# Scores of all nodes kept in SBUF and stored once, and clears and weight loads moved between stages, in a fused graph network

## What is computed

```python
x = _layernorm(x + _L0_gnn_ref(x, edge_index, ...))   # two GAT layers and a matmul with Wu
x = _layernorm(x + _L1_gnn_ref(x, W_fc, attn_l, attn_r, W_res, src, dst))
x = _layernorm(x + _L2_gnn_ref(x, edge_index, W, b))  # GCN
x = _layernorm(x + _L3_gnn_ref(x, W1, b1, W2, b2, edge_index))  # two GCNs

def _L1_gnn_ref(h, ...):
    hh = h.reshape(n, 12, 64)
    ft = einsum('nhd,ed->nhe', hh, W_fc)
    a1, a2 = (ft * attn_l).sum(-1), (ft * attn_r).sum(-1)   # scores of a node: 12 + 12
    e = leaky_relu(a1[src] + a2[dst]); softmax of e over the edges of a target
    return relu(einsum('nhd,ed->nhe', hh, W_res) + sum over edges of alpha * ft[src])
```

## Time and profile before

| | us |
|---|---|
| median of 3 runs | 3817.73 (3816.74 to 3828.18) |
| the profiled execution | 3819.96 |
| its span | 3818.0 |
| TensorE busy in the span | 3544.9 (93%) |
| VectorE | 2428.9 (64%) |
| ScalarE | 1380.7 (36%) |
| GpSimd | 1112.7 (29%) |

### The profile page before, as it was taken

One profiled execution on the slowest core, in us unless ns is written; L12 is line 12 of the kernel. 1 busy time (PEld: TensorE's weight loads), 2 busy tenths in 40 slices (PEclk: granted clock), 3 DMA queues, 4 the chain that ended last, 5 costly groups with the idle time before them and its releaser, 6 DMA issues. The chain is left out here.

```text
span 3818.0 us, 64399 instructions
## 1 busy us (share of the span) xinstructions
PE 3544.9 (93%) x21125; PEld 3356.4 (88%) x21125; DVE 2428.9 (64%) x4799; ACT 1380.7 (36%) x1888; POOL 1112.7 (29%) x1533
## 2 busy tenths in 40 slices
PE   7999999999999999169996999996999998899999
PEld 6999999999999655049995999996999997899999
DVE  4877886148524599338884777775444443677777
ACT  2222232222222355026663444443333333344443
POOL 6540200414521100448883222222222221222221
PEclk9999999999999999589997999998999999999999
DMA  4777987658754698336663333333333333455554
GB/s 114 240 229 217 235 248 244 197 188 254 228 196 150 194 308 284 90 101 215 219 221 122 124 124 128 128 128 135 116 128 124 128 129 141 139 182 181 183 187 144
DMA packets 363376, 672.37 MB, mean 176 GB/s; under 512 B 100181, under 2 KB 193010, under 8 KB 363242
## 3 DMA queue, kind: packets, MB, share of 16 engines
q1 hardware_dynamic: 248154, 441.01, 37.5%
q10 hardware_dynamic: 70160, 155.79, 10.6%
q0 software_dynamic: 44928, 73.84, 6.9%
HBM read 429.79 MB, written 346.94 MB: 203 GB/s over the span
## 5 line engine op out<-in xcount | busy, mean ns | idle before, releaser
L716 DVE TENSOR_TENSOR fr_lo<-fr_turned_ps,fr_hi 128x768 fp32r<-128x768 f32 x158 | 150.4, 952 | 239.2 <-ACT fr_hi L1142 239.2
L2408 DVE SCALAR_TENSOR_TENSOR c3a_y<-c3a_prod,dinv,next_const 128x768 f32<-128x768 f32 x79 | 80.4, 1017 | 288.8 <-PE c3a_prod L2566 288.8
L1286 PE MATMUL fr_prod<-fr_w_hi,fr_hi 128*128 128x396 f32 x948 | 256.8, 352 | 0.0
L1286 PE MATMUL fr_prod<-fr_wu_hi,fr_hi 128*128 128x396 f32 x948 | 254.7, 349 | 0.0
L2566 PE MATMUL cv_prod<-next_w_hi,cv_hi 128*128 128x384 f32 x948 | 249.0, 344 | 0.0
L1286 PE MATMUL fr_prod<-fr_w_lo,fr_hi 128*128 128x396 f32 x948 | 248.9, 344 | 0.0
L2566 PE MATMUL c3a_prod<-next_w_hi,c3a_hi 128*128 128x384 f32 x948 | 248.9, 344 | 0.0
L2566 PE MATMUL c3b_prod<-next_w_hi,c3b_hi 128*128 128x384 f32 x948 | 248.8, 344 | 0.0
L1286 PE MATMUL fr_prod<-fr_w_hi,fr_lo 128*128 128x396 f32 x948 | 248.8, 343 | 0.0
L1286 PE MATMUL fr_prod<-fr_wu_lo,fr_hi 128*128 128x396 f32 x948 | 248.2, 343 | 0.0
L1286 PE MATMUL fr_prod<-fr_wu_hi,fr_lo 128*128 128x396 f32 x948 | 247.7, 342 | 0.0
(11 more groups left out here) (588 smaller groups left out, 9029.2 us busy)
## 6 DMA issues: line engine op xcount, KB each, us to landing
fr_ins<-in_x_dram SPq DMA_DIRECT2D x156, 384.0 KB, 4.3
x<-fr_zrow SPq DMA_DIRECT2D x156, 384.0 KB, 4.9
x<-up_x_o ACTq DMA_DIRECT2D x78, 396.5 KB, 3.9
h<-fr_outs SPq DMA_DIRECT2D x78, 396.0 KB, 3.0
u<-fr_outs SPq DMA_DIRECT2D x78, 396.0 KB, 2.7
up_ut<-u SPq DMA_DIRECT2D x78, 396.0 KB, 4.8
agg<-fr_zrow SPq DMA_DIRECT2D x78, 390.0 KB, 5.9
hds_row<-x SPq DMA_DIRECT2D x78, 384.0 KB, 3.3
```

The source lines that it names most:

```text
L716: v.tensor_tensor(lo[:, s2, :, :], turned_ps[:, 0:KC, :], hi[:, s2, :, :].bitcast(F32), ALU.subtract).then_inc(split_done, 1)
L1286: made = nc.tensor.matmul(prods[s2][:, bank, 0:c1 - c0], l[:, s2, s, :], w[:, s, c0:c1], start=(s == 0 and i == 0), stop=(s == KC - 1 and ...
L2408: v.scalar_tensor_tensor(y3, p3, g["dinv"][:, bass.ds(t, 1)], c3, ALU.mult, ALU.add).then_inc(prod_read, 1)
```

## The change

- In `update_pass` VectorE copies each tile's 25 score columns into a tile `sc_o` that holds all 79, and ScalarE stores it once behind the last tile, lane by lane: the table's row of node i is (i mod 128) * 79 + i div 128. ScalarE's per-tile score store goes.
- Ahead of its tiles VectorE works out where each edge's source and target stand in that table (`place_of`, twice) and clears `sc_o`.
- GpSimd, behind its clear of `rows_x`, clears `w_h`, loads the two weights untransposed, and clears `more`, which is one tile now for all later stages.
- `third_layer` fetches the 20 chunks of target scores first and then the 20 of source rows; VectorE and PE do what needs target scores alone before they wait for the rows.
- `heads_pass` turns the weights with two PE transposes and one ScalarE copy; it has no clears on GpSimd; VectorE clears `rows`, which the first convolution uses.
- `conv_layer` has no clears.

```diff
 update_pass
+            nc.gpsimd.memset(g["w_h"][:, :, :], 0.0).then_inc(w_zero, 1)
+            pool.wait_ge(w_zero, 1)
+            for k, w in enumerate((a["L1_gnn_W_fc"], a["L1_gnn_W_res"])):
+                for q in range(2):
+                    pool.dma_start(g["w_h"][64 * q:64 * q + 64, k, 64 * q:64 * q + 64], w).then_inc(w_in, 16)
+            nc.gpsimd.memset(g["more"][:, :, :], 0.0).then_inc(rows_cleared, 1)
+            pool.wait_ge(w_in, 64)
...
+            def place_of(into, index, k):
+                v.tensor_scalar(into, index, P - 1, None, ALU.bitwise_and).then_inc(placed, 1)
+                v.tensor_scalar(place[:, :], index, 7, None, ALU.arith_shift_right).then_inc(placed, 1)
+                v.tensor_scalar(past[:, :], index, N - 1, FAR, ALU.is_gt, ALU.mult).then_inc(placed, 1)
+                dve.wait_ge(placed, 5 * k + 3)
+                v.scalar_tensor_tensor(into, into, NT, place[:, :], ALU.mult, ALU.add).then_inc(placed, 1)
+                dve.wait_ge(placed, 5 * k + 4)
+                v.tensor_tensor(into, into, past[:, :], ALU.add).then_inc(placed, 1)
+                dve.wait_ge(placed, 5 * k + 5)
+            place_of(g["src_at"][:, :], g["src_i"][:, 0:NC], 0)
+            place_of(g["dst_at"][:, :], g["dst_i"][:, 0:NC], 1)
+            v.memset(sc_o[:, :, :], 0.0).then_inc(sc_cleared, 1)
+            dve.wait_ge(sc_cleared, 1)
...
                 v.scalar_tensor_tensor(x_o[:, slot, D:D + 24], g["v_sum"][:, :], shift[:, s2, :], part[:, s2, :],
                                        ALU.mult, ALU.add).then_inc(scored, 1)
+                dve.wait_ge(scored, t * 2 + 2)
+                v.tensor_copy(sc_o[:, bass.ds(t, 1), :], x_o[:, slot:slot + 1, D:D + 25]).then_inc(kept, 1)
...
-                act.dma_start(tile_rows(sc3, t), x_o[0:n, slot, D:D + 25]).then_inc(stored[slot], 16)
...
+            act.wait_ge(kept, NT)
+            act.dma_start(sc3.rearrange("(p t) w -> p (t w)", p=P), sc_o[:, :, :].rearrange("p t w -> p (t w)")).then_inc(sc_put, 16)
+            act.wait_ge(sc_put, 16)
 third_layer
             for c in range(SC):
+                fetch(sc3, g["dst_at"][:, c:c + 1], at_dst[:, c, :], dst_in, NT * P)
+            for c in range(SC):
                 fetch(x1, g["src_i"][:, c:c + 1], rows[:, c, :], rows_in)
-                fetch(sc3, g["dst_i"][:, c:c + 1], at_dst[:, c, :], dst_in)
...
-            dve.wait_ge(rows_in, 16 * SC)
             dve.wait_ge(dst_in, 16 * SC)
-            link(v.tensor_tensor(z[:, :, :], heads(rows, D), heads(at_dst, H), ALU.add))
             link(v.tensor_tensor(zo[:, :, :], heads(at_dst, 0), heads(at_dst, H), ALU.add))
...
             link(v.tensor_copy(own_r[:, :], pb[0:R, 0:P]))
+            dve.wait_ge(rows_in, 16 * SC)
+            link(v.tensor_tensor(z[:, :, :], heads(rows, D), heads(at_dst, H), ALU.add))
+            v.scalar_tensor_tensor(z[:, :, :], z[:, :, :], SLOPE, z[:, :, :], ALU.mult, ALU.max).then_inc(scored, 1)
+            dve.wait_ge(up, 2)
+            link(v.tensor_copy(zr[:, :], pa[0:R, 0:J * P]))
 heads_pass
-            sp.wait_ge(w_zero, 1)
-            with nc.allow_non_contiguous_dma(reason="small transposed loads"):
-                for k, w in enumerate((a["L1_gnn_W_fc"], a["L1_gnn_W_res"])):
-                    for q in range(2):
-                        sp.dma_start(w_st[64 * q:64 * q + 64, k, 64 * q:64 * q + 64], w.rearrange("e d -> d e")).then_inc(w_in, 16)
...
-            nc.gpsimd.memset(w_st[:, :, :], 0.0).then_inc(w_zero, 1)
-            nc.gpsimd.memset(more[:, :, :], 0.0).then_inc(cleared, 1)
-            pool.wait_ge(cleared, 1)
...
-            dve.wait_ge(cleared, 1)
+            v.memset(g["rows"][:, :, :], 0.0).then_inc(cleared, 1)
             own(0, 0, 0)
...
+            act.wait_ge(w_up, 1)
+            nc.scalar.activation(w_st[:, :, :].rearrange("p k c -> p (k c)"), prods[0][:, 0, 0:2 * P], ACT.Copy).then_inc(w_turned, 1)
...
-            pe.wait_ge(w_in, 64)
+            for k in range(2):
+                made = nc.tensor.transpose(prods[0][:, 0, k * P:(k + 1) * P], g["w_h"][:, k, :], g["ident"][:, :])
+            made.then_inc(w_up, 1)
+            pe.wait_ge(w_turned, 1)
 conv_layer
-            if first:
-                pool.wait_ge(cleared, 2)
...
-            if first:
-                v.memset(rows[:, :, :], 0.0).then_inc(cleared, 1)
-                v.memset(more[:, :, :], 0.0).then_inc(cleared, 1)
```

More of the change, by code:

```diff
@@ L173, in build @@
         first_layers(nc, g, a, packed, packed2, sources, agg, h1, sc1, h2, out2, u, x2, x3)
+        g["more"], g["w_h"] = sb("more", [P, UNROLL, AGG_W]), sb("w_h", [P, 2, P])
         with ExitStack() as mid:
@@ L178, in build @@
             g["alpha"], g["own_w"] = mid_sb("alpha", [P, NC, H_MAX]), mid_sb("own_w", [P, NC, H_MAX])
-            update_pass(nc, g, u, out2, x1, sc3)
+            g["src_at"], g["dst_at"] = mid_sb("src_at", [P, NC], I32), mid_sb("dst_at", [P, NC], I32)
+            update_pass(nc, g, a, u, out2, x1, sc3)
             third_layer(nc, g, x1, sc3, agg)
+        g["rows"] = sb("rows", [P, S2, D])
         heads_pass(nc, g, a, x1, agg, x2[0:N, :])
@@ L184, in build @@
         g["w_const"] = sb("next_const", [P, D])
-        g["more"], g["rows"] = sb("more", [P, UNROLL, D]), sb("rows", [P, S2, D])
-        conv_layer(nc, g, "cv", x2, x3[0:N, :], a["L2_gnn_W"], a["L2_gnn_b"], res=x2, first=True)
+        conv_layer(nc, g, "cv", x2, x3[0:N, :], a["L2_gnn_W"], a["L2_gnn_b"], res=x2)
         conv_layer(nc, g, "c3a", x3, x2[0:N, :], a["L3_gnn_W1"], a["L3_gnn_b1"])
@@ L1450, in update_pass @@
         x_o = sb("x_o", [P, UNROLL, D + 25])
+        sc_o = sb("sc_o", [P, NT, 25])
+        place, past = sb("place", [P, NC], I32), sb("past", [P, NC], I32)
         part, scrap = sb("part", [P, 2, 24]), sb("scrap", [P, 1])
@@ L1514, in shift_of @@
                 if at_least(t, UNROLL):
-                    dve.wait_ge(stored[slot], turn * 32)
+                    dve.wait_ge(stored[slot], turn * 16)
                 v.tensor_copy(x_o[:, slot, D + 24:D + 25], g["own"][:, bass.ds(t, 1)]).then_inc(scored, 1)
@@ L1548, in polish @@
                 if at_least(t, UNROLL):
-                    act.wait_ge(stored[slot], turn * 32)
+                    act.wait_ge(stored[slot], turn * 16)
                 nc.scalar.activation(x_o[:, slot, 0:D], y[:, slot, 0:D], ACT.Identity, bias=shift[:, s2, :],
@@ L1673, in _, with fetch @@
         def _(pool):
-            def fetch(table, index, into, done):
+            def fetch(table, index, into, done, rows=N):
                 nc.gpsimd.indirect_dma_start(into, None, table, bass.IndirectOffsetOnAxis(ap=index, axis=0),
-                                             bounds_check=N - 1, oob_is_err=False).then_inc(done, 16)
+                                             bounds_check=rows - 1, oob_is_err=False).then_inc(done, 16)
             def store(index, j, done):
@@ L1693, in scores @@
                 for j in range(GROUP):
-                    fetch(sc3, ix[:, 0, j:j + 1], got[:, 0, j, :], a_in)
-                    fetch(sc3, ix[:, 1, j:j + 1], got[:, 1, j, :], a_in)
+                    fetch(sc3, ix[:, 0, j:j + 1], got[:, 0, j, :], a_in, NT * P)
+                    fetch(sc3, ix[:, 1, j:j + 1], got[:, 1, j, :], a_in, NT * P)
                 pool.wait_ge(a_in, r * (32 * GROUP) + 32 * GROUP)
@@ L1966, in _ @@
                 hs = slice(j * HG, (j + 1) * HG)
-                nc.tensor.transpose(pa[0:R, j * P:(j + 1) * P], z[:, hs, :].rearrange("p h c -> p (h c)"), ident[:, :])
                 nc.tensor.transpose(pa[0:R, 256 + j * P:256 + (j + 1) * P], zo[:, hs, :].rearrange("p h c -> p (h c)"), ident[:, :])
             nc.tensor.transpose(pb[0:R, 0:P], own6[:, :, :].rearrange("p h c -> p (h c)"), ident[:, :]).then_inc(up, 1)
+            pe.wait_ge(scored, 2)
+            for j in range(J):
+                hs = slice(j * HG, (j + 1) * HG)
+                made = nc.tensor.transpose(pa[0:R, j * P:(j + 1) * P], z[:, hs, :].rearrange("p h c -> p (h c)"), ident[:, :])
+            made.then_inc(up, 1)
             for k in (1, 2):
@@ L2042, in heads_pass @@
         sem = semaphores(nc, ctx, "hds_")
-        row, more = sb("row", [P, UNROLL, D]), sb("more", [P, UNROLL, AGG_W])
+        row, more = sb("row", [P, UNROLL, D]), g["more"]
         ix = sb("ix", [P, UNROLL], I32)
@@ L2243, in _, with conv_layer @@
             over_tiles(pe, step, 1)
-def conv_layer(nc, g, tag, table, out, weights, bias, res=None, first=False, last=False):
+def conv_layer(nc, g, tag, table, out, weights, bias, res=None, last=False):
     with ExitStack() as ctx:
@@ L2259, in conv_layer @@
         res_in = sb("res", [P, UNROLL, D]) if apart else rows_in
-        more, rows = g["more"], g["rows"]
+        more, rows = g["more"][:, :, 0:D], g["rows"]
         scrap_s = sb("scrap_s", [P, 3])
@@ L2279, in conv_layer @@
         stored = [sem(f"stored{j}") for j in range(UNROLL)]
```

(2 more changed lines are left out.)

18 lines of the change are left out of this document (8 added, 10 removed).

## The result

The changed kernel takes 3849.5 us (median of four runs, 3846.9 to 3854.7); the kernel before, timed beside it, 3821.8. The ratio is 1.0074 (95% interval 1.0060 to 1.0088): slower by 28 us. Forecast were 3828 us and +9.9, in a range that ended at 3840. The profiled execution took 3854.66 us, its span is 3852.5.

What follows compares the result with a forecast made beforehand. VectorE was taken to bound the update pass; between stages each wait counts one to one. 19 + 8 + 2.6 - 3.3 - 8.6 - 7.8 = +9.9 on 3817.73 gave 3828 us, range (8 in 10) 3806 to 3840.

Steps and rivals of the forecast that it cites:

- The copy, +19: Update pass: waiting for L1519 and copying scores on VectorE adds 0.24 us a tile over 79 tiles, +19 us.
- slow copy: Rival, update pass: L1496 can't overlap the copy or the computed address holds it; 0.37 a tile, +20, 3838; chance 0.20.
- the base: What the sum was added to: profiled execution 3819.96 us; median of three timed runs 3817.73.
- upper end, +29: Update pass, score copy: 0.26 to the next start and 0.16 now, 0.37 us a tile, +29 us.
- Lists, +8: Before VectorE's first update tile: list operations wait out GpSimd's rows_x memset, then clearing; first tile 7.4 later, +8 us taken.
- VectorE isn't held: Rival, start of update pass: GpSimd's memset doesn't block VectorE's list operations; +1.9 in total, 3820; chance 0.20.
- Nobody waits: Update pass: GpSimd's further clears and four small loads follow behind 1291.6, end long before 1530, hold nobody.
- Bulk store, +2.6: End of update pass: storing all scores once, 1.01 MB at 387 GB/s, adds 2.6 us.
- Third layer, -3.3: Start of third layer: target scores first gains 4.1 us, a bigger last fetch loses up to 0.8; -3.3.
- Heads, -8.6: Start of heads pass: weight loads and GpSimd memsets leave their queues, so L2101 starts at +5.8, not 14.4; -8.6 us.
- First convolution, -7.8: Start of first convolution: without two clears its seam takes 26.4 us like the second's, not 34.2; -7.8.
- PE sets the pace: Rival, update pass: PE, busy 9.96 of 10, is the bound, so the copy hides; -9, 3809; chance 0.10.

Runs made afterwards that it cites:

- the seams: Changed kernel with per-tile score stores as before, no copy, lists or clearing on VectorE; target scores first, TensorE weight turns, rings cleared in passing stay: 3811.4 us, ratio 0.9962.
- the late copy: Against the changed kernel, VectorE copies the previous tile's scores, behind the scaling into part: 3825.3 us.

## Why the prediction was wrong

The sum was +9.9, the stages give +24.6 without their first line. By its own steps:

1. *The copy, +19.* This step failed. The place was right (VectorE's end of tile, with L1524 and in the end PE behind it) and so were three of its pieces: 0.244 for the scaling, 0.03 for a link, 0.12 to 0.20 for the copy to the next start. Missing was the address of sc_o's column, which I left out of the sum and named only among the rivals ("or the address computed for each tile holds it"). It stands behind the wait, and cost 0.136 of the 0.377 us a tile, 10.6 us (inside the loop, without the slow third product, 0.131 of 0.382). The 0.03 came from a linked pair at the kernel's start, outside any loop and with constant addresses, and was used for an instruction whose address comes from a register. The rival "slow copy" had the size, 0.37, and one of its two causes, the address; the other, that L1496 can't overlap the copy, is refuted by the 0.12 above. It had 0.20, and its 3838 is still 11 us short, since it has neither the last convolution nor the base in it. The step's own upper end, +29, is the measured figure, but by that refuted cause; that they meet is luck.
2. *Lists, +8.* Measured +8.0, by the lock that was given. The part of it put down to PE's low clock was filled by idle time ahead of the clearing, and the low clock itself showed two tiles later, in the line of the pass. "VectorE isn't held" is refuted. "Nobody waits" for GpSimd's further clears held in the changed kernel only because its tiles began so late; once they begin early, it costs some 2 us.
3. *Bulk store, +2.6.* +2.3.
4. *Third layer, -3.3.* -3.0, in part by luck: up to the scan 2.3 are gained (to the end of the last issue 0.35 lost, behind it 2.6 gained), and 0.7 more behind the scan, which no step had. The 0.8 for the bigger last fetch was an estimate without a row; the landing came 1.1 later.
5. *Heads, -8.6.* -7.4. The term mis-sized is the landing of the first index fetch, 4.9 us behind its issue instead of 2 to 3.4; the upper bound would have been nearer. That the row loads beside it hold it up was only argued. VectorE's clearing didn't hold GpSimd.
6. *First convolution, -7.8.* -6.9, just outside the ends given (-7 and -8); 26.9 against 26.4 to the last put, the rest not looked for.

"PE sets the pace" is refuted: a copy added to VectorE lengthened each tile. It may not be far off, though. Without the copy a tile takes 3.00 us with PE busy 9.96 of 10, so a further saving on VectorE would probably soon meet it; no run shows this.

To the steps come +2.5 in the last convolution, which no step had, and the base. The median of 3817.73 was that of three runs; beside the later kernels 21 runs gave 3824.5. The profile on which the sum was built had the shortest way to the update pass of the ten. The 28 us between the medians are the 24.6 of the stages and some 3 that this variation can hold; of the 21.5 us between 3828 and 3849.5 the steps and the last convolution explain 14.7 (24.6 - 9.9). For the rest the base and the variation of the first stage are the explanation at hand; it isn't shown for the timed runs, of which no stage is known.

## What to carry to other kernels

An instruction that waits for the one before it on its own engine costs the rest of that one, a link, and, if its address comes from a register, the work on that address too; give it to an engine with slack, or do it one tile late, under a wait that is there anyway: here 0.377, 0.067 or no time a tile for the same copy. Small integer operations of VectorE can stand behind a long memset of GpSimd for its whole length (13.4 us here); let them go first, where GpSimd's work has time, and then look which other small operations its clears now fall beside (2.1 us here). And where an edit removes transfers nobody waits for and adds work on the engine that sets the pace, its best outcome is no loss: the seams were worth having (12 us), and alone they were at least as fast as with the scores on chip.

## What was not expected of the hardware

The 0.147 us of idle time in front of a waiting VectorE copy whose destination is addressed by a register, against 0.035 with a constant one; behind a met wait the same register instruction shows no idle time (0.0 before the late copy). The lock that, once avoided at the start of the pass, came back two tiles later beside a shorter GpSimd clearing. And the 8 us by which one and the same program reaches its update pass earlier or later: one wait of 2.4 to 8.3 us early on, which makes up a part of it, with the clock at 0.96 down to 0.86 in the stretch behind it.
